# Second attention: weighing with the values standing in quarters of the array, and the order of VectorE's first counts and maxima

## The chip, the cores and the metric

One core of a Trainium2 chip runs the whole program. The metric is the device time of one execution in microseconds. Each kernel is run several times, and the median is taken. One more execution is recorded by the hardware profiler.

## The reference

Four transformer layers run one after the other on x of 8 batches, 256 tokens and 128 features, each an attention and a feed-forward stage behind an adaptive layer norm. The change lies in the attention of the second layer, here "the second attention":

```python
scores = einsum('bhqd,bhkd->bhqk', q, k) / sqrt(8)       # 16 heads of 8 features
attn = softmax(scores)
keep = rank_of(attn) < k_keep[head]                      # the k_keep largest of each row of 256
w = where(keep, attn, 0)
w = w / (sum(w) + 1e-10)
out = einsum('bhqk,bhkd->bhqd', w, v) @ Wo.T + bo
```

`k_keep` is a number per head, worked out from two small inputs. The other seven stages are untouched, but for two semaphores of the second layer pair's feed-forward stage that get another name.

## The kernel before

Every stage has its work written out by hand for each engine, in a fixed order, and the engines meet through semaphores. TensorE is PE in the rows, VectorE DVE, ScalarE ACT and GpSimd POOL.

**The second attention** is a pipeline over the batches. The loop `for n in range(-1, B)` stands in `l1_attn` of each engine. In the pass of n the engines work on four batches at once: n is weighed, n+1 has its thresholds searched, n+2 gets its scores, maxima and exponentials, and n+3 is projected. A batch has 16 heads and 2 tiles of 128 queries, so 32 blocks ("rows" in the code) of 128 queries by 256 keys.

- **The search** finds for each row of attention a threshold with k_keep values above it, up to a window of 8. It counts three times: VectorE counts six blocks (`count_below`, L3085), ScalarE the other 26 (`l1_count`, L4235). Behind the first count VectorE works out the next threshold in `first_move` (L3093), behind the second and third in `narrow` (L3105). Each of them waits until ScalarE has ended its counts. Then VectorE takes the final count with flags (`count_kept`, L3156), and `doubt` (L3168 to L3172) counts the rows whose count missed the window.
- **The doubts.** TensorE sums these over the partitions (`l1_doubt`, L1765). VectorE copies the sum to an integer (`ask_doubt`, L3177, then a memset L3179), loads it into a register and branches (`settle_doubt`): over a long bisection that is not needed with these inputs, to a line that raises two semaphores. Behind it `settle_doubt` writes `past` (L3192) and raises `over_ready`, which TensorE's `l1_turn` (L1671) waits for.
- **The marks.** Of each group of 4 blocks `largest_of` takes the eight largest candidates (MAX8, L3200), `all_but_past` (L3206) leaves those that are too many, and `mark` (L3212) marks them. `mark(n, 0)` needs `past`.
- **Turning and weighing.** `l1_turn_probs` (L1744, L1745) turns the probabilities of a head and takes away what is marked, and ScalarE's `l1_take_probs` (L4246) brings them to SBUF as `probsT`, in two buffers that take turns. `l1_weigh` (L1758) multiplies: for each of 2 query tiles and 2 key tiles the 128x128 piece of `probsT` is loaded as the standing operand, and 9 columns (8 of the values and a one, which gives the sum) move through. An f32 product is two instructions, so a head is eight. The result lies in bank 1 with the queries in the partitions.
- **The end of a batch.** VectorE's `weighed` (L3222 to L3226) divides by the sum, `l1_turn_out` and `l1_project_out` (L1778) project, and `l1_result` (L3233) hands over to GpSimd.
- **The order of a pass.** On VectorE the pass of n began with `largest_of(n, 0)`, `largest_of(n, 1)`, `ask_doubt(n)`, `settle_doubt(n)`, `all_but_past`, `mark(n, 0)`, then `l1_max(n+2, 0)` (L3072), `count_below(n+1, 0)`, `first_move(n+1)` and `weighed(n-1)`. On TensorE it begins with `l1_doubt(n)`, directly behind `l1_weigh(n-1, 15)`. On ScalarE it begins with the last of batch n+1's first counts, from block 20 on.

The waits of `l1_take_probs(b, h)`: for the turned head, and for `l1_weigh(b, h-2)`, which frees the buffer. ScalarE's exponentials of head h (`l1_exps`, L4185) wait for `l1_max` of that head on VectorE.

Of the kernel before, what the change touches and what calls it, by code (L numbers as in the profile page):

```python
# [11 lines left out]
ALU = mybir.AluOpType  # L12
# [3 lines left out]
P = 128  # L16
B, S, D = 8, 256, 128
T = S // P
H = 16
# [39 lines left out]
GROUP_WORDS = 4 * S // 2  # L59

# [124 lines left out]
def adaln_program(nc, x_in, c_in, const_in, ali_in, weights_in, out):  # L185
    ctx = ExitStack()
    with ctx:
# [287 lines left out]
        minus_two = silu_b[:, 0:P // 2].bitcast(BF16)  # L475
        first_rows = front_n[:].rearrange("p t d -> p (t d)")
# [131 lines left out]
        z_psum = signal("z_psum", l2_ffn=1)  # L608
        z_ready = signal("z_ready", l2_ffn=1)
# [645 lines left out]
        def _(pe):  # L1255
# [492 lines left out]
            def l1_weigh(b, h, ph="l1_attn"):  # L1748
# [5 lines left out]
                wide = HD + 1  # L1754
                for t in range(T):
                    for k in range(T):
                        at = t * S + k * P
                        last = mm(pb[1][:, t * S + h * wide:t * S + (h + 1) * wide], probsT[:, h % 2, at:at + P],  # L1758
                                  values_of(b, k)[:, h * wide:(h + 1) * wide], start=k == 0, stop=k == T - 1)
                last.then_inc(pv_done.sem, 1)  # L1760
# [20 lines left out]
            def l1_attn(ph="l1_attn"):  # L1781
# [10 lines left out]
                for n in range(-1, B):  # L1792
                    if now(n):
                        l1_doubt(n)
                    if now(n + 2):
                        l1_values(n + 2)
# [36 lines left out]
                    if now(n):  # L1833
                        l1_weigh(n, 4)
# [40 lines left out]
                    if now(n):  # L1875
                        l1_turn_probs(n, 13)
                        l1_weigh(n, 11)
                        l1_weigh(n, 12)
                        l1_turn_probs(n, 14)
# [3 lines left out]
                        l1_weigh(n, 15)  # L1883
                l1_turn_out(B - 1)
# [171 lines left out]
            def l2_fall(p, ph="l2_ffn"):  # L2056
# [3 lines left out]
                last.then_inc(z_psum.sem, 1)  # L2060

            def l2_out(p, ph="l2_ffn"):

                pe.wait_ge(pass_done.sem, pass_done(ph, p, 1))
                pe.wait_ge(z_ready.sem, z_ready(ph, p, 1))
# [240 lines left out]
        def _(dve):  # L2306
# [908 lines left out]
            def weighed(b, ph="l1_attn"):  # L3215
                dve.wait_ge(pv_done.sem, pv_done(ph, b, H))
                if b:
                    dve.wait_ge(turned.sem, turned(ph, b - 1, 1))
                wide = H * (HD + 1)
                o1 = tiles(pb[1])[:, :, 0:wide].rearrange("p t (h d) -> p t h d", h=H)  # L3220
                sums_by_tile = sums_of(b).rearrange("p h t -> p t h")
                link(V_.scalar_tensor_tensor(kept_sum, sums_by_tile, 1e-10, o1[:, :, :, HD], ALU.mult, ALU.add))  # L3222
# [3 lines left out]
                V_.tensor_tensor(tokens1.rearrange("p t (h d) -> p t h d", h=H), o1[:, :, :, 0:HD],  # L3226
# [1451 lines left out]
```

## Time and profile before

| | |
|---|---|
| median of 3 runs | 2046.71 us (2041.7 to 2064.53) |
| the profiled execution | 2043.58 us, of which span 2041.8 us |
| busy share of the span: PE, DVE, ACT, POOL | 80%, 72%, 55%, 43% |
| the second attention | about 493 to 1109 us of the span |
| one pass of it, in the middle | 70.4 to 71.0 us |

The busy shares are over stages with different limits. The second attention must be read from its own passes.

### The profile page before, as it was taken

How to read it: one execution, taken by the hardware profiler on the slowest of the kernel's cores; microseconds unless marked ns; L12 is line 12 of the kernel's file. 1: busy time of each engine (PE TensorE's matmuls, PEld its weight loads, DVE VectorE, ACT ScalarE, POOL GpSimd, SP SyncE). 2: the span in 40 equal slices, each digit the busy share in tenths (PEclk: the TensorE clock that was granted, in tenths of full speed). 3: DMA queues.
4: the chain of work that ended last, by engine and by line, in shares of the span. 5: the costliest groups of instructions: out<-in, count | busy, mean ns of one | idle time of the engine just before them, and what ended most of it. 6: DMA issues, size and time to landing. Idle time of an engine off the chain costs nothing.

```text
span 2041.8 us, 38862 instructions
## 1 busy us (share of the span) xinstructions
PE 1642.0 (80%) x12640; PEld 1172.7 (57%) x12640; DVE 1476.3 (72%) x4747; ACT 1115.7 (55%) x3322; POOL 877.4 (43%) x1162
## 2 busy tenths in 40 slices
PE   3888989897358988988779978527777799999978
PEld 3445667675236766766668645413443477777763
DVE  6678776555588988999887842358876777887657
ACT  2444444445988898899852423214452366666620
POOL 3333221124253554444433577676300377767610
PEclk8889999997555555555557989858896899999969
DMA  4111101003000000000001023322110000000000
GB/s 139 47 47 41 40 21 42 18 2 122 15 9 17 12 13 11 17 9 9 1 1 59 23 78 110 97 65 73 48 72 20 15 1 1 2 1 2 1 1 21
DMA packets 67305, 67.58 MB, mean 33 GB/s; under 512 B 9955, under 2 KB 58966, under 8 KB 66566
## 3 DMA queue, kind: packets, MB, share of 16 engines
q1 hardware_dynamic: 58930, 53.09, 7.9%
q0 software_dynamic: 5120, 10.50, 2.0%
q8 instruction: 104, 1.70, 0.4%
q10 hardware_dynamic: 3040, 1.38, 0.2%
q14 instruction: 111, 0.91, 0.2%
HBM read 30.41 MB, written 8.39 MB: 19 GB/s over the span
## 4 chain that ended last, share of the span: by engine, by line
PE 35%; DVE 27%; ACT 12%; issue 10%; POOL 6%; SPq 6%; ACTq 2%; DMA 1%; DVEq 0%; POOLq 0%
SPq L689 5%; POOL weights L1165 4%; DVE weights L3212 3%; PE bank L2143 3%; PE bank L1551 3%; PE bank L2103 3%; ACT big L4445 3%; PE bank L1567 3%; DVE weights L3156 3%; DVE nmax L3072 2%; DVE small L3200 2%; PE bank L1758 2%; PE bank L2130 2%; ACT rope_s L4235 2%; ACT rope_c L4235 2%
## 5 line engine op out<-in xcount | busy, mean ns | idle before, releaser
L1758 PEld LDWEIGHTS bank<-V,probsT 128*128 128x128 f32 x1024 | 203.6, 297 | 28.4 <-ACT probsT L4246 13.7
L1758 PE MATMUL bank<-V,probsT 128*128 128x9 f32 x1024 | 205.4, 333 | 15.2 <-ACT probsT L4246 10.9
L2711 DVE TENSOR_REDUCE nmax<-bank 128x4 f32<-128x1024 f32 x144 | 175.9, 1221 | 51.8 <-PE bank L1331 48.8
L891 POOL TENSOR_TENSOR big<-big,rinv 128x512 f32<-128x512 f32 x128 | 131.7, 1049 | 45.7 <-DVE rinv L3767 45.7
L1745 PE MATMUL bank<-silu_b,weights 128*128 128x128 bf16 x464 | 138.9, 303 | 0.0
L4050 ACT ACTIVATE feat_o<-bank 128x1024 f32<-128x1024 f32 x72 | 73.7, 1023 | 101.5 <-PE bank L1331 66.7
L4050 ACT ACTIVATE O<-bank 128x1024 f32<-128x1024 f32 x72 | 73.7, 1024 | 97.2 <-PE bank L1331 70.6
L3761 DVE TENSOR_REDUCE nmax<-bank 128x2 f32<-128x512 f32 x128 | 81.9, 682 | 58.1 <-PE bank L2103 58.1
L4445 ACT ACTIVATE big<-bank,nmax 128x256 f32<-128x256 f32 x256 | 117.6, 478 | 11.1 <-DVE nmax L3761 11.1
L4453 ACT ACTIVATE big<-bank 128x512 f32<-128x512 f32 x128 | 73.8, 614 | 68.8 <-PE bank L2130 68.8
L4246 ACT ACTIVATE probsT<-bank 128x512 f32<-128x512 f32 x128 | 75.9, 600 | 58.4 <-PE bank L1745 39.0
L1165 POOL DMA_INDIRECT weights<-h_rows,V x96 | 91.7, 955 | 32.2 <-issue 28.9
L1729 PE MATMUL bank<-qT 48*128 48x256 bf16 x256 | 62.8, 387 | 44.1 <-ACT weights L4185 34.2
L1744 PE MATMUL bank<-const,big 128*128 128x128 f32 x256 | 86.4, 417 | 8.7 <-DVE weights L3212 7.7
L3072 DVE TENSOR_REDUCE nmax<-bank 128x2 f32<-128x512 f32 x128 | 84.1, 681 | 9.3 <-PE bank L1729 9.3
L2143 PE MATMUL bank<-big,V 128*64 128x256 f32 x512 | 69.4, 390 | 16.9 <-ACT V L4460 15.7
L3537 DVE TENSOR_TENSOR O<-O,bank 128x512 f32<-128x512 f32 x24 | 16.5, 687 | 90.1 <-ACT O L4369 82.9
L4109 ACT ACTIVATE hid<-bank,weights 128x256 f32<-128x256 f32 x128 | 52.5, 470 | 48.5 <-PE bank L1551 48.4
L2130 PE MATMUL bank<-const,big 128*128 128x128 f32 x512 | 75.0, 279 | 2.5 <-POOL big L891 1.7
L1744 PEld LDWEIGHTS bank<-const,big 128*128 128x128 f32 x256 | 59.4, 232 | 29.6 <-DVE weights L3212 9.9
L1173 POOL DMA_INDIRECT weights<-y_rows,V x64 | 61.8, 966 | 29.8 <-issue 16.9
L2130 PEld LDWEIGHTS bank<-const,big 128*128 128x128 f32 x512 | 56.6, 141 | 29.0 <-issue 16.5
(818 smaller groups left out, 5110.5 us busy)
## 6 DMA issues: line engine op xcount, KB each, us to landing
qT<-parts SPq DMA_DIRECT2D x276, 32.0 KB
big<-V SPq DMA_DIRECT2D x192, 32.0 KB
y_rows<-weights SPq DMA_DIRECT2D x24, 256.0 KB, 2.3
big<-parts SPq DMA_DIRECT2D x180, 32.0 KB
weights<-in_weights_l_ffn SPq DMA_DIRECT2D x1, 4832.0 KB, 14.3
weights<-in_weights_l_attn SPq DMA_DIRECT2D x1, 3904.0 KB, 13.0
qT<-V SPq DMA_DIRECT2D x96, 32.0 KB
weights<-in_weights_l_ffn SPq DMA_DIRECT2D x1, 2860.0 KB, 11.7
```

Source lines behind the costliest of these rows:

```text
L689: queue.dma_start(stacks[m % STACKS][to, u * HALF:(u + 1) * HALF], pair_of(m, at, *of)).then_inc(stack_in[u].sem, 16)
L891: nc.gpsimd.tensor_tensor(row, row, rinv[:, h % H, :].unsqueeze(2).to_broadcast([P, T, S]), ALU.mult).then_inc(scaled.sem, 1)
L1165: nc.gpsimd.indirect_dma_start(gathered[i % RING1][:, t, :], None, h_rows, bass.IndirectOffsetOnAxis(ap=token_of[:, at:at + 1], axis=0)).t ...
L1744: mm(pb[6 + h % 2][:, at], row_of(b, 2 * h + t)[:, keys], C("ident"), start=True, stop=False, is_transpose=True)
L1745: last = mm(pb[6 + h % 2][:, at], unkept(b, g)[:, 2 * (h % 2) + t, keys], minus_two, start=False, stop=True)
L1758: last = mm(pb[1][:, t * S + h * wide:t * S + (h + 1) * wide], probsT[:, h % 2, at:at + P], values_of(b, k)[:, h * wide:(h + 1) * wide], s ...
L2130: last = nc.tensor.transpose(pb[TURN_BANKS3[h % 2]][:, k * S + t * P:k * S + (t + 1) * P], probs3[h % PROBS3][:, t * S + k * P:t * S + (k ...
L2143: last = mm(pb[7][HD3 * i:HD3 * (i + 1), w * S:(w + 1) * S], values3(q, k, 2 * w + i), probsT3[(4 * q + 2 * w + i) % TURNED3][:, k * S:(k ...
L2711: V_.tensor_reduce(to, scored.rearrange("p (i a n) -> p i a n", i=HPG, n=n), AX.X, ALU.max, negate=True).then_inc(score_max.sem, 1)
L3072: V_.tensor_reduce(nmax[:, h, :], tiles(pb[2 + n % 3]), AX.X, ALU.max, negate=True).then_inc(max_ready.sem, 1)
L4050: nc.scalar.activation(turned_probs[n % TURNS], turned_scores, ACT.Exp).then_inc(turned_exp.sem, 1)
L4445: last = nc.scalar.activation(probs3[h % PROBS3][:, t * S:(t + 1) * S], pb[h % 4][:, t * S:(t + 1) * S], ACT.Exp, bias=nmax[:, h % H, t:t ...
```

## The change

Three things, all in the second attention.

1. `l1_weigh` has the operands the other way round: the values of a head (128 keys x 9) stand, in the column quarter `h % 4` of the array, and the 256 queries of `probsT` move. Two products per head instead of four, four instructions instead of eight. The result has the features in the partitions: four heads share columns 0 to 255 of bank 1.
2. So every four heads ("a quad") ScalarE copies these 256 columns to SBUF (`l1_take_quad`), and TensorE turns them back with two products (`l1_turn_quad`), where the standing operand is 128x128 of the copy and 36 columns of the identity move. The first three quads go to columns 256 on of bank 1, the last to columns 0 on. The next quad's first `l1_weigh` stands behind `l1_turn_quad` on TensorE, and that waits for the copy. The last quad is copied and turned at the start of the next pass, behind `l1_doubt`. `weighed` reads two places, so it has five instructions instead of three.
3. On VectorE the pass begins with `count_below(n+1, 0)`, then `ask_doubt(n)`, then the eight maxima of `largest_of`, then `settle_doubt(n)`.

On TensorE `l1_turn_probs(n, 14)` moves ahead of `l1_weigh(n, 12)`.

```diff
+        weighed_quad = V[:, 0, 576:576 + S]
+        early_heads = 3 * H // 4
+        weighed_at = ((slice(0, early_heads), pb[1][:, S:S + T * early_heads * (HD + 1)]),
+                      (slice(early_heads, H), pb[1][:, 0:T * (H - early_heads) * (HD + 1)]))
...
-        z_psum = signal("z_psum", l2_ffn=1)
-        z_ready = signal("z_ready", l2_ffn=1)
+        side_psum = signal("side_psum", l1_attn=QUADS, l2_ffn=1)
+        side_taken = signal("side_taken", l1_attn=QUADS, l2_ffn=1)
...
             def l1_weigh(b, h, ph="l1_attn"):
...
-                for t in range(T):
-                    for k in range(T):
-                        at = t * S + k * P
-                        last = mm(pb[1][:, t * S + h * wide:t * S + (h + 1) * wide], probsT[:, h % 2, at:at + P],
-                                  values_of(b, k)[:, h * wide:(h + 1) * wide], start=k == 0, stop=k == T - 1)
+                wide, part = HD + 1, slice(32 * (h % 4), 32 * (h % 4) + HD + 1)
+                by_keys = probsT[:, h % 2, :].rearrange("p (t k n) -> p k t n", t=T, k=T)
+                for k in range(T):
+                    last = mm(pb[1][part, 0:S].rearrange("p (t n) -> p t n", t=T), values_of(b, k)[:, h * wide:(h + 1) * wide], by_keys[:, k],
+                              start=k == 0, stop=k == T - 1)
                 last.then_inc(pv_done.sem, 1)
+
+            def l1_turn_quad(b, q, ph="l1_attn"):
+                pe.wait_ge(side_taken.sem, side_taken(ph, b, q + 1))
+                of_heads = C("ident").rearrange("p (j d) -> p j d", j=4)[:, :, 0:HD + 1]
+                heads_there, there = weighed_at[q // 3]
+                at = 4 * q - heads_there.start
+                for t in range(T):
+                    o = there.rearrange("p (t h d) -> p t h d", t=T, d=HD + 1)[:, t, at:at + 4, :]
+                    last = mm(o, weighed_quad[:, t * P:(t + 1) * P], of_heads, start=True, stop=True)
+                last.then_inc(side_psum.sem, 1)
...
                     if now(n):
                         l1_doubt(n)
+                    if now(n - 1):
+                        l1_turn_quad(n - 1, QUADS - 1)
...
+                        l1_turn_quad(n, 0)
                         l1_weigh(n, 4)
...
                         l1_turn_probs(n, 10)
+                        l1_turn_quad(n, 1)
                         l1_weigh(n, 8)
...
                         l1_turn_probs(n, 13)
                         l1_weigh(n, 11)
+                        l1_turn_probs(n, 14)
+                        l1_turn_quad(n, 2)
                         l1_weigh(n, 12)
-                        l1_turn_probs(n, 14)
                         l1_turn_probs(n, 15)
                         l1_weigh(n, 13)
...
                 for n in range(-1, B):
+                    if now(n + 1):
+                        count_below(n + 1, 0)
                     if now(n):
+                        ask_doubt(n)
                         largest_of(n, 0)
                         largest_of(n, 1)
-                        ask_doubt(n)
                         settle_doubt(n)
                         all_but_past(n, 0)
                         mark(n, 0)
                     if now(n + 2):
                         l1_max(n + 2, 0)
                     if now(n + 1):
-                        count_below(n + 1, 0)
                         first_move(n + 1)
...
+            def l1_take_quad(b, q, ph="l1_attn"):
+                act.wait_ge(pv_done.sem, pv_done(ph, b, 4 * q + 4))
+                nc.scalar.activation(weighed_quad, pb[1][:, 0:S], ACT.Copy).then_inc(side_taken.sem, 1)
...
                         l1_count(n + 1, 0, 20, 21)
+                    if now(n - 1):
+                        l1_take_quad(n - 1, QUADS - 1)
...
+                        l1_take_quad(n, 0)
                         l1_take_probs(n, 5)
...
+                        l1_take_quad(n, 1)
                         l1_take_probs(n, 9)
...
                         l1_exps(n + 2, 14)
                     if now(n):
+                        l1_take_quad(n, 2)
                         l1_take_probs(n, 14)
```

## Rows read from the trace of the kernel before

**Rows 1.** The page, part 2: the granted TensorE clock in 40 equal slices.

```profile
PEclk8889999997555555555557989858896899999969
```

**Rows 2.** Window of one pass: busy PE, PEld, DVE, ACT, POOL, then granted clock.

```profile
862.40:932.80 70.40, 63.20 (x322) 50.66 (x322) 64.23 (x268) 63.30 (x243) 33.03 (x42) 0.54 0.04 13
```

**Rows 3.** Timeline of DVE at a pass's start: start, length, line, idle before.

```profile
862.32 0.19 DVE L3172 TENSOR_SCALAR_CACHE_REDUCE small<-small 128x32 f32<-128x32 f32 x1
862.43 2.71 DVE L3200 MAX8 small<-hid 128x8 f32<-128x256 f32 x8
866.10 0.14 DVE L3177 CAST doubts_i<-bank 1x1 int32<-1x1 f32 x1 [0.96 <-PE bank L1765]
...
870.01 0.42 DVE L3192 TENSOR_TENSOR weights<-const,small 128x256 f32<-128x256 f32 x1 [3.64 <-DVEq L3189]
...
872.91 0.47 DVE L3085 TENSOR_SCALAR_CACHE_REDUCE scale_b<-weights,front_n 128x256 bf16<-128x256 f32 x1
...
875.52 0.19 DVE L3093 TENSOR_TENSOR front_n<-front_n,routes 128x32 f32<-128x32 f32 x1
```

**Rows 4.** Timeline of DVE: the same instruction as the first, one pass later.

```profile
932.70 0.19 DVE L3172 TENSOR_SCALAR_CACHE_REDUCE small<-small 128x32 f32<-128x32 f32 x1
```

**Rows 5.** Timeline of PE at the same pass's start; heads 14 and 15 turned first.

```profile
857.15 0.45 PE L1744 MATMUL bank<-const,kT 128*128 128x128 f32 x1
...
859.91 1.82 PE L1758 MATMUL bank<-V,probsT 128*128 128x9 f32 x8
862.36 3.58 PE L1758 MATMUL bank<-V,probsT 128*128 128x9 f32 x16 [0.62 <-ACT probsT L4246]
865.87 0.19 PE L1765 MATMUL bank<-main_square,ones 128*1 128x1 f32 x2
...
870.58 0.66 PE L1671 MATMUL bank<-const,xb 128*128 128x128 f32 x2 [3.37 <-DVE weights L3192]
```

**Rows 6.** Timeline of ACT: exponentials of head 13, `l1_take_probs` 14, a 128x256 copy.

```profile
854.36 0.47 ACT L4185 ACTIVATE O<-bank,nmax 128x256 f32<-128x256 f32 x1 [2.13 <-DVE nmax L3072]
...
861.72 0.58 ACT L4246 ACTIVATE probsT<-bank 128x512 f32<-128x512 f32 x1
...
881.67 0.38 ACT L4215 ACTIVATE feat<-bank 128x256 f32<-128x256 f32 x1
```

**Rows 7.** Timelines of ACT and DVE: ends of second and third counts, `narrow` behind each.

```profile
891.15 0.21 ACT L4235 ACTIVATION_READ_ACCUMULATOR rope_s<-kT,small 128x1 f32 x1
...
892.62 0.19 DVE L3105 TENSOR_TENSOR small<-small,routes 128x32 f32<-128x32 f32 x1
...
910.08 0.54 ACT L4235 ACTIVATE rope_c<-kT,small 128x256 bf16<-128x256 f32 x1
...
911.92 0.18 DVE L3105 TENSOR_TENSOR small<-small,routes 128x32 f32<-128x32 f32 x1
```

**Rows 8.** Timeline of PE: f32 products of other shapes, in this stage and in others.

```profile
906.92 0.87 PE L1702 MATMUL bank<-probs,kT 128*128 128x16 f32 x4
907.64 1.85 PE L1758 MATMUL bank<-V,probsT 128*128 128x9 f32 x8
...
1855.65 1.03 PE L2091 MATMUL bank<-next_feat,weights 128*128 128x256 f32 x4
1856.52 1.03 PE L2114 MATMUL bank<-weights,feat 128*128 128x256 f32 x4
...
309.08 0.64 PE L1404 MATMUL bank<-O,big 128*32 128x256 f32 x8
309.65 2.05 PE L1519 MATMUL bank<-const 128*128 128x128 f32 x16
```

**Rows 9.** Timeline of PE in the last pass: the clock granted is full here.

```profile
1086.70 1.91 PE L1758 MATMUL bank<-V,probsT 128*128 128x9 f32 x16
```

**Rows 10.** Windows behind TensorE's restart at 870.58, with the granted clock.

```profile
870.00:876.00 6.00, 5.17 (x26) 3.51 (x27) 5.75 (x27) 4.78 (x19) 0.00 (x0) 0.50 0.00 1
876.00:877.00 1.00, 0.79 (x3) 0.29 (x2) 0.93 (x5) 1.00 (x4) 0.63 (x3) 0.89 0.00 0
```

More of the change, by code:

```diff
@@ L59 @@
 GROUP_WORDS = 4 * S // 2
+QUADS = H // 4
 QUICK_STEPS = 3
@@ L1753, in l1_weigh @@
                 pe.wait_ge(probsT_ready.sem, probsT_ready(ph, b, h + 1))
-                wide = HD + 1
-                for t in range(T):
-                    for k in range(T):
-                        at = t * S + k * P
-                        last = mm(pb[1][:, t * S + h * wide:t * S + (h + 1) * wide], probsT[:, h % 2, at:at + P],
-                                  values_of(b, k)[:, h * wide:(h + 1) * wide], start=k == 0, stop=k == T - 1)
-                last.then_inc(pv_done.sem, 1)
+                wide, part = HD + 1, slice(32 * (h % 4), 32 * (h % 4) + HD + 1)
[3 more added lines that the diff above has]
+                              start=k == 0, stop=k == T - 1)
+                last.then_inc(pv_done.sem, 1)
+            def l1_turn_quad(b, q, ph="l1_attn"):
[3 more added lines that the diff above has]
+                at = 4 * q - heads_there.start
+                for t in range(T):
+                    o = there.rearrange("p (t h d) -> p t h d", t=T, d=HD + 1)[:, t, at:at + 4, :]
+                    last = mm(o, weighed_quad[:, t * P:(t + 1) * P], of_heads, start=True, stop=True)
+                last.then_inc(side_psum.sem, 1)
             def l1_doubt(b, ph="l1_attn"):
@@ L1883, in l1_attn @@
                         l1_weigh(n, 15)
+                l1_turn_quad(B - 1, QUADS - 1)
                 l1_turn_out(B - 1)
@@ L2059, in l2_fall @@
                     last = mm(pb[6][:], W(ph, "win2")[:, c * P:(c + 1) * P], gelus(c), start=c == 0, stop=c == O2 - 1)
-                last.then_inc(z_psum.sem, 1)
+                last.then_inc(side_psum.sem, 1)
             def l2_out(p, ph="l2_ffn"):
                 pe.wait_ge(pass_done.sem, pass_done(ph, p, 1))
-                pe.wait_ge(z_ready.sem, z_ready(ph, p, 1))
+                pe.wait_ge(side_taken.sem, side_taken(ph, p, 1))
                 for j in range(2 * T):
@@ L3215, in weighed @@
             def weighed(b, ph="l1_attn"):
-                dve.wait_ge(pv_done.sem, pv_done(ph, b, H))
+                dve.wait_ge(side_psum.sem, side_psum(ph, b, QUADS))
                 if b:
                     dve.wait_ge(turned.sem, turned(ph, b - 1, 1))
-                wide = H * (HD + 1)
-                o1 = tiles(pb[1])[:, :, 0:wide].rearrange("p t (h d) -> p t h d", h=H)
                 sums_by_tile = sums_of(b).rearrange("p h t -> p t h")
-                link(V_.scalar_tensor_tensor(kept_sum, sums_by_tile, 1e-10, o1[:, :, :, HD], ALU.mult, ALU.add))
+                for of, there in weighed_at:
+                    o1 = there.rearrange("p (t h d) -> p t h d", t=T, d=HD + 1)
+                    link(V_.scalar_tensor_tensor(kept_sum[:, :, of], sums_by_tile[:, :, of], 1e-10, o1[:, :, :, HD], ALU.mult, ALU.add))
                 linkup()
@@ L3225, in weighed @@
                 linkup()
-                V_.tensor_tensor(tokens1.rearrange("p t (h d) -> p t h d", h=H), o1[:, :, :, 0:HD],
-                                 kept_sum.unsqueeze(3).to_broadcast([P, T, H, HD]), ALU.mult).then_inc(tok_ready.sem, 1)
+                for of, there in weighed_at:
+                    o1 = there.rearrange("p (t h d) -> p t h d", t=T, d=HD + 1)
+                    heads_there = of.stop - of.start
+                    last = V_.tensor_tensor(tokens1.rearrange("p t (h d) -> p t h d", h=H)[:, :, of], o1[:, :, :, 0:HD],
+                                            kept_sum[:, :, of].unsqueeze(3).to_broadcast([P, T, heads_there, HD]), ALU.mult)
+                    if of.stop == H:
+                        last.then_inc(tok_ready.sem, 1)
+                    else:
+                        link(last)
             def l1_result(b, ph="l1_attn"):
@@ L4347, in l1_attn @@
                         l1_count(n + 2, 0, 17, 20)
+                l1_take_quad(B - 1, QUADS - 1)
                 l1_take_out(B - 1)
@@ L4424, in l2_ffn @@
             def l2_ffn(p, ph="l2_ffn"):
-                act.wait_ge(z_psum.sem, z_psum(ph, p, 0))
+                act.wait_ge(side_psum.sem, side_psum(ph, p, 0))
                 for c in range(O2):
```

4 lines of the change are left out of this document (2 added, 2 removed).

## The prediction

> **What bounds the kernel now.** I read the clock by slices first, then one middle pass of the second attention in the windows, then VectorE's timeline at its start, then TensorE's and ScalarE's. The clock stands at its lower level, 1.2 GHz, almost throughout this stage [rows 1], so TensorE's prices here are doubled. In a pass of 70.4 us three engines are nearly full: TensorE 63.2 us, VectorE 64.2, ScalarE 63.3 [rows 2]. No busy share names the bound; the waits do. Call D the moment when VectorE has the doubts counted and starts the eight maxima (862.43), and P the moment when TensorE's sum of them is there (866.10). VectorE needs 2.7 us for the maxima, waits 0.96 us for P, and behind the copy stands idle 3.64 us for the load and the branch [rows 3]. These 4.6 us are nearly all its idle time in a pass. P is late because TensorE still weighs heads 14 and 15 until 865.9, and it had waited 0.62 us for ScalarE to bring head 14 [rows 5]. ScalarE had waited 2.13 us for VectorE's maximum of head 13, some 8 us before D [rows 6]. So the loop is VectorE, ScalarE, TensorE, VectorE.
>
> ScalarE has little room elsewhere. It ends its second counts at 891.36 and its third at 910.6, and VectorE comes for them at 892.62 and 911.92 [rows 7]: 1.3 us of slack each.
>
> **VectorE's order.** Before, from D to `first_move` it is 13.1 us (862.43 to 875.52) [rows 3]: maxima, wait, copy, branch, `past`, marks, `l1_max`, and last `count_below` with 2.6 us (872.91 to 875.52). After, `count_below` covers the wait instead of the maxima, and the maxima run while the sequencer loads and branches. From P to `first_move` it was 9.4 us; without the count 6.8, and 0.1 for issuing eight maxima: 6.9. The time from D is then (P-D) + 6.9, as long as P-D is over 2.6. With P-D at 3.67 as before this would be 10.6, a gain of 2.5 us a pass. It is lost once P-D reaches 6.2. That the sequencer goes on while maxima are queued isn't shown by a row of a branch; bounds are 0 and 2.7 us covered, and I take the full cover, as nothing behind the maxima waits for them before `past`.
>
> **What weighing costs.** A head is now 4 instructions with 256 moving columns. In the fourth layer four f32 instructions of that shape follow each other in 0.87 us at full clock (1855.65 to 1856.52) [rows 8], so 1.74 at half. Before, a head was half of 3.5 us at half clock [rows 5] and half of 1.9 minus the tail, 0.88, at full [rows 9]. So turning the operands round saves TensorE nothing: it was bound by loading 128 columns eight times, and is bound now by moving 256 four times. Changing between the whole array and a quarter: in the first attention eight such instructions in four quarters take 0.57 us (309.08 to 309.65) [rows 8] where two rounds of 0.22 are 0.43; so 0.1 each time, taken as 0.13 for a head. New is `l1_turn_quad`, four instructions with a 128-column load: the nearest row has four with 16 columns in 0.72 (906.92 to 907.64) [rows 8], I take 0.9 at half clock. Per pass +3.6 and +2.0, on 63.2: TensorE would be full in 69 us at the lower clock.
>
> ScalarE gets four copies of 0.38 us [rows 6]. VectorE gets two more small instructions in `weighed`, 0.2 us. The renamed semaphores cost nothing: the same waits. No DMA and no queue of SP or GpSimd is passed by a moved step.
>
> **The new handshake, where I see the price.** `l1_take_quad(n, 2)` stands behind ScalarE's exponentials of head 14, where `l1_take_probs` 14 started at 861.72 [rows 6]. ScalarE can't come sooner: it waits for VectorE's maximum of head 13, and works from there without a pause. The copy ends at 862.1, D minus 0.3. Only then may TensorE turn the quad, and behind this in its queue stand weigh 12, turn 15, and weigh 13, 14 and 15, and then the doubts' sum. Before, only 14 and 15 were left at this time. At half clock: 0.9 + 1.87 + 1.38 (two heads were turned in 2.76, 857.15 to 859.91 [rows 5]) + 1.87 + 3.6 = 9.6 us, so P-D = -0.3 + 9.6 + 0.2 = 9.4. At full clock half of it, P-D = 4.7. ScalarE waits too: `l1_take_probs` 14 needs weigh 12, and `l1_take_quad` 3 needs weigh 15.
>
> The clock: 256 columns now move where 9 did, and stages with such weighing have it full [rows 1], so I expect it to be full in more of the pass. But TensorE, having turned head 14, stands idle for the copy, several us at full clock. Behind the like pause at 870.58 it ran at the lower level until about 876 [rows 5, 10], 5.5 us. I take that: 5.5 us of the 9.6 at half, the other 4.1 in 2.05. P-D = 7.4. Then `first_move` is at D + 14.3, 1.2 later than before.
>
> **What is late next.** ScalarE goes on only from P, and needs 44.5 us from P to the end of its third counts (866.10 to 910.6) [rows 3, 7]; plus 0.5 for copies and the later start. VectorE would be at its `narrow` sooner behind P than before and waits. From there it has 20.9 us to the next D [rows 4, 7]. So a pass is P-D + 44.5 + 0.5 + 0.1 + 20.9 = P-D + 66.0: 73.4 us, 3.0 more than 70.4.
>
> **The sum**, against the profiled execution (2043.58 us, 3.1 under the median of 2046.71). Five passes, n = 1 to 5, have everything: +15.0. In n = 6 ScalarE has no exponentials and only the 1.2 + 0.2 count: +1.4. Pass 0 has no weighing ahead of its doubts, so the cover works, but ScalarE's slack of 1.3 less one copy lets through 0.9: -0.9. The doubts of pass 7: -2.0 of the 2.7. Behind them TensorE alone sets the end. There 14 or so heads at full clock cost 0.13 more, three quads 0.5 each, and copy, turn and two waits 1.2 at the end; against it the clock rises some us sooner: -1.8 (from -2.3 to +20, were it to stay low). In all +11.7: **2055 us**.
>
> Against this stands a rule of the Trainium skill (TensorEngine Tiling (Array Packing), Key Properties): tiles in different columns load and multiply in parallel. By it heads 13, 14 and 15, in three quarters and next to each other, would overlap. It is a rival below. The same list says that changing the tiling mode drains the engine; the row puts that at 0.1 us, so it changes little.
>
> **Rivals.**
> - *The clock stays low* (slower; 0.22). A product in one quarter may not lift it. P-D = 9.4, a pass 75.4: five times 5.0, pass 6 +6.2 as TensorE is full there, -0.9, -2.0: +28, 2072 us. It decides from P-D = 6.2 up. For it: this stage alone never had the clock. Against: the other weighing stages have it.
> - *The branch isn't covered* (slower; 0.08). `first_move` at P + 9.6, a pass 74.5, and passes 0 and 7 lose their gain: +23, 2067 us.
> - *Full clock at once* (0.12). P-D = 4.7, a pass 70.7: five times 0.3, pass 6 -1.3, -0.9, -4.3: 2039 us.
> - *The quarters overlap* (0.07). Eight instructions in 0.57 us [rows 8] instead of 1.74 show what neighbours can do. Three heads in the time of one, 3.6 us less at half clock: P-D = 5.6, a pass 71.6: +0.5, 2044 us. Against: each head's four stay in one quarter.
> - *The handshake isn't late* (faster; 0.13). Were ScalarE at its copy 4 us earlier, P-D would be 2.6 or less. ScalarE's counts are then the bound: 0.7 to 1.9 us less a pass: five times 1.9, pass 6 -3.6, -0.9, -4.3: -18, 2025 us.
>
> **How the numbers follow.** The forecast has 0.38. A change within 1% (20 us) can't be told from none here. Faster by more needs the last rival and something beside it, 0.14 with what I may have missed. Slower by more, over 2067: most of the low clock, half of the uncovered branch, some of the forecast's upper part: 0.27. The rest, 0.59, is within. The range goes from the fast rival to the low clock with part of the last pass: 2026 to 2080.
>
> **What would show it.** After: L1765 some 7 us behind D instead of 3.7, with VectorE's wait for it 4 us or more; a wait of ScalarE at L4246 for L1758 of about 3 us in front of head 14; idle time between the maxima and L3192 of about 1.3 us instead of 3.64; small waits at L3105; the clock above 0.55 in the pass. Wrong would be the forecast if ScalarE's copy of quad 2 comes well ahead of D, if TensorE has the full clock when it arrives, or if VectorE's maxima end long before L3192.

## Result and profile after

The changed kernel takes 2066.73 us, the median of 20 runs (2060.29 to 2071.63), beside 2050.95 us (2041.06 to 2064.53, 20 runs) for the kernel before: a ratio of 1.008, 95% interval 1.0063 to 1.0096. The profiled execution took 2064.9 us, its span 2063.1. The forecast was 2055 us, within 1%.

The page's clock by slices ([rows 1] has those of before), and from its costliest groups the weighing, the turn of a quarter (new) and `l1_take_probs` with the idle time ahead of them. (A "quarter" of the heads is the quad of the code, which counts from 0: quad 2 is the third quarter, heads 8 to 11.)

```profile
PEclk9899999997567777777688989857887899999969
...
L1762 PE MATMUL bank<-probsT,V 128*9 128x256 f32 x512 | 157.4, 469 | 23.3 <-ACT probsT L4274 23.0
...
L4274 ACT ACTIVATE probsT<-bank 128x512 f32<-128x512 f32 x128 | 76.2, 601 | 74.0 <-PE bank L1762 53.9
...
L1773 PE MATMUL bank<-const,V 128*128 128x36 f32 x128 | 29.3, 368 | 82.5 <-ACT V L4278 82.5
```

TensorE's mean granted clock over the stage is 0.73 now instead of 0.57, and it stands 82.5 us in all for ScalarE's copies of the quarters. The windows of the whole stage (busy PE, PEld, DVE, ACT, POOL, then clock), before:

```profile
480.00:1135.00 655.00, 521.19 (x2758) 415.43 (x2757) 557.96 (x2288) 521.66 (x1959) 276.70 (x354) 0.57 0.07 23
```

and after:

```profile
480.00:1135.00 655.00, 434.68 (x2268) 231.64 (x2266) 541.69 (x2259) 520.69 (x1969) 270.90 (x350) 0.73 0.06 21
```

TensorE is 87 us less busy, and the kernel is slower. VectorE's timeline of pass 4, the counterpart of [rows 3]: the doubts' count, the copy of their sum, the maxima, `past`, `first_move`, the narrowings, and the maxima of later scores.

```profile
868.88 0.18 DVE L3192 TENSOR_SCALAR_CACHE_REDUCE small<-small 128x32 f32<-128x32 f32 x1
...
876.28 0.15 DVE L3197 CAST doubts_i<-bank 1x1 int32<-1x1 f32 x1 [4.80 <-PE bank L1779]
...
876.59 2.71 DVE L3220 MAX8 small<-hid 128x8 f32<-128x256 f32 x8
880.46 0.43 DVE L3212 TENSOR_TENSOR weights<-const,small 128x256 f32<-128x256 f32 x1 [1.16 <-DVEq L3209]
...
884.99 0.19 DVE L3113 TENSOR_TENSOR front_n<-front_n,routes 128x32 f32<-128x32 f32 x1 [1.54 <-ACTq L4267]
...
902.50 0.19 DVE L3125 TENSOR_TENSOR small<-small,routes 128x32 f32<-128x32 f32 x1 [0.55 <-ACTq L4267]
...
922.11 0.19 DVE L3125 TENSOR_TENSOR small<-small,routes 128x32 f32<-128x32 f32 x1 [0.24 <-ACTq L4267]
...
926.04 1.29 DVE L3092 TENSOR_REDUCE nmax<-bank 128x2 f32<-128x512 f32 x2 [1.01 <-PE bank L1734]
```

These six waits are 9.30 us. The pass takes 75.13 us (868.88 to 944.01), so 65.83 without them. Before, it took 70.38 with 4.60 of waits [rows 3, 4], 65.78 without. **A pass is VectorE's 65.8 us and its waits**, in both kernels. The branch's cover works (1.16 instead of 3.64), but the wait for the sum grew from 0.96 to 4.80, and four waits came up that weren't there.

TensorE at the same place, to be held against [rows 5]: turn of quad 2, weigh 12, weigh 13 and 14 together, the first product of weigh 15, turn of quad 3.

```profile
868.73 1.07 PE L1773 MATMUL bank<-const,V 128*128 128x36 f32 x4 [7.58 <-ACT V L4278]
869.73 1.88 PE L1762 MATMUL bank<-probsT,V 128*9 128x256 f32 x4
...
873.01 1.43 PE L1762 MATMUL bank<-probsT,V 128*9 128x256 f32 x8
875.17 0.39 PE L1762 MATMUL bank<-probsT,V 128*9 128x256 f32 x1 [0.74 <-ACT probsT L4274]
...
878.79 0.64 PE L1773 MATMUL bank<-const,V 128*128 128x36 f32 x4 [2.59 <-ACT V L4278]
```

And ScalarE, against [rows 6]: copy of quad 2, `l1_take_probs` 14 and 15, copy of quad 3, its last count.

```profile
868.30 0.37 ACT L4278 ACTIVATE V<-bank 128x256 f32<-128x256 f32 x1
871.70 0.60 ACT L4274 ACTIVATE probsT<-bank 128x512 f32<-128x512 f32 x1 [3.03 <-PE bank L1762]
...
874.52 0.60 ACT L4274 ACTIVATE probsT<-bank 128x512 f32<-128x512 f32 x1 [1.74 <-PE bank L1762]
...
878.37 0.37 ACT L4278 ACTIVATE V<-bank 128x256 f32<-128x256 f32 x1
...
884.32 0.50 ACT L4263 ACTIVATE rope_c<-kT,front_n 128x256 bf16<-128x256 f32 x1
```

TensorE stands 7.58 us for a copy that ends at 868.67, 0.2 before the doubts' count. ScalarE then stands 3.03 and 1.74 us for TensorE, and only behind that come its counts, the last at 884.8, just ahead of `first_move`. Two windows of TensorE behind its restart, in the columns as above; the clock was at 0.50 from 864 on:

```profile
870.00:872.00 2.00, 2.00 (x7) 0.69 (x6) 1.48 (x8) 0.30 (x1) 0.00 (x0) 0.50 0.00 0
...
874.00:876.00 2.00, 1.26 (x10) 0.38 (x6) 0.00 (x0) 1.48 (x6) 0.00 (x0) 1.00 0.00 0
```

### The profile page after: what moved, and what is told of

Its sections match the earlier page's. It is cut to its first block, busy times and chain, and to the rows that moved or that the text cites. A ratio compares the mean times of both kernels' runs of the same rounds, so it can differ in the third digit from the quotient of the medians.

```text
span 2063.1 us, 38143 instructions
## 1 busy us (share of the span) xinstructions
PE 1575.1 (76%) x12256; PEld 1003.5 (49%) x12256; DVE 1481.8 (72%) x4763; ACT 1125.2 (55%) x3354; POOL 877.6 (43%) x1162
## 4 chain that ended last, share of the span: by engine, by line
PE 36%; ACT 23%; DVE 17%; issue 9%; POOL 6%; SPq 5%; ACTq 2%; DMA 1%; DVEq 0%; POOLq 0%
ACT rope_s L4263 5%; ACT rope_c L4263 5%; SPq L694 5%; POOL weights L1170 4%; PE bank L2163 3%; PE bank L2123 3%; ACT big L4483 3%; PE bank L1556 3%; PE bank L1572 3%; DVE weights L3176 3%; PE bank L1762 2%; PE bank L2150 2%; DVE nmax L2731 2%; PE bank L2111 2%; ACT big L4213 2%
## 5 line engine op out<-in xcount | busy, mean ns | idle before, releaser
L1762 PE MATMUL bank<-probsT,V 128*9 128x256 f32 x512 | 157.4, 469 | 23.3 <-ACT probsT L4274 23.0
L1750 PE MATMUL bank<-silu_b,weights 128*128 128x128 bf16 x464 | 110.7, 259 | 0.0
L1773 PE MATMUL bank<-const,V 128*128 128x36 f32 x128 | 29.3, 368 | 82.5 <-ACT V L4278 82.5
L1734 PE MATMUL bank<-qT 48*128 48x256 bf16 x256 | 52.1, 340 | 45.2 <-ACT weights L4213 32.6
L1762 PEld LDWEIGHTS bank<-probsT,V 128*9 128x9 f32 x512 | 38.3, 101 | 93.9 <-issue 40.2
L3565 DVE TENSOR_TENSOR O<-O,bank 128x512 f32<-128x512 f32 x24 | 16.5, 688 | 90.2 <-ACT O L4407 78.3
L2150 PE MATMUL bank<-const,big 128*128 128x128 f32 x512 | 75.1, 279 | 2.5 <-POOL big L896 1.7
L1749 PE MATMUL bank<-const,big 128*128 128x128 f32 x256 | 69.7, 353 | 7.4 <-DVE weights L3232 3.8
L1360 PE MATMUL bank<-big 57*128 57x128 bf16 (+1 forms) x512 | 42.7, 271 | 38.2 <-DVE nmax L2731 24.2
```

Of the source, the lines that this page charges most:

```text
L1750: last = mm(pb[6 + h % 2][:, at], unkept(b, g)[:, 2 * (h % 2) + t, keys], minus_two, start=False, stop=True)
L1762: last = mm(pb[1][part, 0:S].rearrange("p (t n) -> p t n", t=T), values_of(b, k)[:, h * wide:(h + 1) * wide], by_keys[:, k], start=k == 0, ...
L2150: last = nc.tensor.transpose(pb[TURN_BANKS3[h % 2]][:, k * S + t * P:k * S + (t + 1) * P], probs3[h % PROBS3][:, t * S + k * P:t * S + (k ...
```

## Experiments

In the table D is the start of the doubts' count, P that of the copy of their sum (VectorE's timelines), the stage the time from the first D to the eighth; distances are of pass 4. Ratios are to the kernel before, measured beside each.

| kernel | median us | ratio, interval | stage | P-D | `first_move`-D |
|---|---|---|---|---|---|
| before | 2050.95 | | 484.5 | 3.78 | 13.2 |
| changed | 2066.73 | 1.008, 1.0063 to 1.0096 | 511.0 | 7.40 | 16.1 |
| e1 VectorE's order alone | 2050.32 | 0.9986, 0.9955 to 1.0016 | 482.7 | 2.51 | 10.6 |
| e2 weighing alone | 2074.15 | 1.0117, 1.0076 to 1.0157 | 510.9 | 7.50 | 17.0 |
| e3 third copy early | 2030.84 | 0.9913, 0.9884 to 0.9942 | 477.4 | 2.97 | 10.9 |
| e4 wait filled | 2048.92 | 0.9985, 0.9956 to 1.0014 | 493.0 | 5.08 | 13.8 |
| e5 counts, exponentials ahead | 2074.55 | 1.011, 1.0068 to 1.0152 | 515.4 | 8.89 | 16.2 |
| e6 sum ahead | 2069.76 | 1.0097, 1.0062 to 1.0132 | 510.0 | 2.51 | 16.5 |
| e7 e5 and e6 | 2067.11 | 1.0084, 1.0053 to 1.0115 | 506.1 | 2.51 | 16.0 |
| e8 e3, old order | 2038.58 | 0.994, 0.9914 to 0.9966 | 480.7 | 2.74 | 12.1 |
| e9 counts ahead | 2063.52 | 1.0074, 1.0047 to 1.01 | 507.4 | 7.42 | 14.5 |
| e10 e9 and e6 | 2055.86 | 1.0033, 1.0009 to 1.0058 | 497.8 | 2.52 | 14.4 |
| e12 before, last pass filled | 2048.35 | 1.0011, 0.9986 to 1.0036 | 484.0 | 3.78 | 13.2 |
| e13 e3, second copy early | 2035.56 | 0.9926, 0.9898 to 0.9954 | 475.2 | 2.52 | 10.8 |

**The two parts apart.** To the kernel before only VectorE's new order was given:

```diff
+                    if now(n + 1):
+                        count_below(n + 1, 0)
                     if now(n):
+                        ask_doubt(n)
                         largest_of(n, 0)
                         largest_of(n, 1)
-                        ask_doubt(n)
                         settle_doubt(n)
...
-                        count_below(n + 1, 0)
                         first_move(n + 1)
```

> The kernel before with VectorE's new order alone: the first count and the doubts' count, then the two maxima, then the doubts' copy and the branch; TensorE's and ScalarE's programs are those of before. Theory A (the order gives its cover, but the pass is then held by ScalarE's counts and by TensorE's scores): the idle time of the branch falls from 3.64 to about 1.2 us a pass, first_move starts 1 to 2.5 us sooner after the doubts' count, and the whole comes out 5 to 12 us under the kernel before, 2039 to 2046. Rival B (the branch was hidden by nothing and everything behind it moves up): 2.5 us a pass more than that is not to be had, but all of 3.64 - 1.16 = 2.5 us in each of 7 passes is, 17 us, 2034. Rival C (the handoff of the doubts is late in any order): no change, 2051.

`first_move` comes 2.6 us sooner in pass 4, but the stage is only 1.8 us shorter and the whole can't be told from before. The median is rival C's, but not for its reason: in passes 1, 3, 5 and 6 P-D is 3.8 to 4.3, much as before (2.9 to 4.3), and yet `first_move` comes 1.3 to 3.8 us sooner in each pass but pass 3, whose branch is long (below). A's gain is there and is mostly waited away: in pass 4 waits for ScalarE of 0.91 and 0.59 and one of 0.69 for TensorE take its place. Passes 1, 2 and 4 are 1.2 to 1.8 us shorter than before, pass 3 is 2.0 longer. Then the changed kernel with the old order (the same diff backwards):

> The changed kernel with VectorE's old order (maxima first, then the doubts' count, the branch, then the first count), so the weighing change alone. Theory A (the quarter's turn on TensorE holds up the doubts' sum, and the new order wins back about 1 to 2.5 us a pass of it): the wait for the doubts' sum is 4 to 6 us as the doubts' count comes later, first_move comes 1 to 2.5 us a pass later than in the changed kernel, the whole is 5 to 12 us over it, 2072 to 2079. Rival B (once TensorE is the late one, VectorE's order is worth nothing): within 2 us of the changed kernel, 2067.

```profile
882.57 0.15 DVE L3197 CAST doubts_i<-bank 1x1 int32<-1x1 f32 x1 [4.68 <-PE bank L1779]
...
886.51 0.43 DVE L3212 TENSOR_TENSOR weights<-const,small 128x256 f32<-128x256 f32 x1 [3.66 <-DVEq L3209]
...
932.33 1.29 DVE L3092 TENSOR_REDUCE nmax<-bank 128x2 f32<-128x512 f32 x2 [1.01 <-PE bank L1734]
```

These are all its waits in pass 4, 9.35 us beside the changed kernel's 9.30. The stage is 510.9 us beside 511.0: in it the new order is worth nothing, which is B's mechanism. It turned 2.5 us of branch into 2.3 us of waiting for ScalarE. But the median is 7.4 us over the changed kernel's, which is A's range and not B's. The profiled spans differ by 8.8 us: 6.1 lie before the first D, 1.5 in the last pass (from D to `weighed` 41.9 us instead of 40.4), 1.3 behind it. The 6.1 need not be the order's, for two profiles with the same code up to there, of the kernel before and of e12, have their first D at 578.1 and at 571.8. So the order's worth in the whole stays open: nothing in passes 0 to 6 of these profiles, 1.5 us in the last.

**The late copy.** One call moved on ScalarE:

```diff
                         l1_exps(n + 2, 13)
+                    if now(n):
+                        l1_take_quad(n, 2)
+                    if now(n + 2):
                         l1_start(n + 2)
...
                     if now(n):
-                        l1_take_quad(n, 2)
                         l1_take_probs(n, 14)
```

> The changed kernel with one call moved on ScalarE: the copy of the third quarter (heads 8 to 11) stands right behind the exponentials of head 13, ahead of the counts 5 to 14, instead of behind those of head 14. Theory A (the loss is the 7.5 us in which TensorE stands before the turn of the quarter, the probabilities of head 15 and the doubts' sum behind it): that idle time is gone, the doubts' sum comes about 3 us after VectorE's count instead of 7.4 to 8.2, the pass falls from 75.4 to about 70 us and the whole is 25 to 35 us under the changed kernel, 2032 to 2042. Rival B (the low clock under quarters is what is late, the wait only takes its place): the wait is gone but the turns and weighings of heads 12 to 15 still run at half clock for 6 to 7 us, a gain of 5 to 10 us, 2057 to 2062. Rival C (the counts on ScalarE set the pass): the copy's wait moves to ScalarE and the counts end no sooner, within 3 us of the changed kernel.

VectorE's first three waits in pass 4 (0.78, 0.24 and 1.01 follow, 4.28 in all beside 9.30):

```profile
852.53 0.15 DVE L3197 CAST doubts_i<-bank 1x1 int32<-1x1 f32 x1 [0.38 <-remote]
...
856.72 0.42 DVE L3212 TENSOR_TENSOR weights<-const,small 128x256 f32<-128x256 f32 x1 [1.16 <-DVEq L3209]
...
860.41 0.19 DVE L3113 TENSOR_TENSOR front_n<-front_n,routes 128x32 f32<-128x32 f32 x1 [0.71 <-ACTq L4267]
```

A holds, at 1 us under its range: the whole is 36 us below the changed kernel and, by its own comparison, 0.6 to 1.2% below the kernel before. So the copy's place carries all of the loss. e8 is e3 with VectorE's old order:

> The kernel with the third quarter's copy moved forward, with VectorE's old order (maxima, doubts' count, branch, then the first count): the weighing by quarters without the late copy and without VectorE's new order. Theory A (with the copy in time, VectorE is late, and its new order is worth what it covers of the branch less what it then waits for ScalarE): idle before the pass's second tile of work is 3.7 us instead of 1.2, no wait for ScalarE at first_move and at the narrowings (0.71, 0.78, 0.24 before), so 0.6 to 1.2 us a pass more, the whole 3 to 9 us over the 2031 of the kernel with the early copy, 2034 to 2040. Rival B (the new order is worth all of the 2.5 us that it covers): 17 us over it, 2048.

7.7 us over e3 by the medians, 3.3 in the stage: A by its total. With the copy in time, VectorE's order is worth something, though not the 2.5 us a pass that it covers, and not A's 0.6 to 1.2 us in each pass: 2.9 of the 3.3 lie in pass 1, where the branch is long (below).

**Clock or order?** On TensorE, between the turn of head 14 and that of the quarter, products whose result nobody reads:

```diff
                         l1_turn_probs(n, 14)
+                        if now(n + 2):
+                            for _ in range(28):
+                                mm(pb[0][:, 0:P], C("ident"), C("ident"), start=True, stop=True)
                         l1_turn_quad(n, 2)
```

> The changed kernel with 28 products of the identity by itself (128 x 128, into a bank of the scores, read by nobody) on TensorE between the turn of head 14 and the turn of the quarter, in each pass where they fit: they fill some 2 to 3 us of the 7.5 us in which TensorE stands there, so that the clock has less idle time before the heads 12 to 15. Theory A (the clock's part of the handoff is small beside the order's): the copy by ScalarE comes no sooner, the handoff gets 0 to 2 us shorter where the clock is at 1.00, the whole comes out 0 to 12 us under the changed kernel, 2055 to 2067. Rival B (the clock is the main part): the handoff falls from 7.5 to about 5 us, 17 us and more under it, 2050 or less.

TensorE in pass 4: the useless products, the turn of quad 2, weigh 12, weigh 13 and 14.

```profile
857.03 6.47 PE L1899 MATMUL bank<-const 128*128 128x128 f32 x56
864.79 0.64 PE L1773 MATMUL bank<-const,V 128*128 128x36 f32 x4 [1.28 <-ACT V L4281]
865.35 1.03 PE L1762 MATMUL bank<-probsT,V 128*9 128x256 f32 x4
...
867.15 1.04 PE L1762 MATMUL bank<-probsT,V 128*9 128x256 f32 x8
```

My theory A misses: it is B that holds. The products fill 6.47 of the 7.58 us, not the 2 to 3 that I expected, and the granted clock stays at 1.00 from 857.0 to 870.0 in this profile. The copy comes no sooner, yet P-D falls by 2.32 us, since the same work runs at 2.4 GHz (1.03 for weigh 12 instead of 1.88). Of the 3.62 us by which P-D had grown, 2.3 are the price of restarting at 1.2 GHz behind the idle time. The pass is 3.2 us shorter, since the maxima's later wait of 1.01 goes too. With 28 useless products in a pass the kernel is 18 us faster than the changed one.

**Is the sum of the doubts the late one?** On TensorE the sum goes ahead of the turn of the quarter:

```diff
-                    if now(n):
+                    if n == 0:
                         l1_doubt(n)
...
                         l1_turn_probs(n, 14)
+                        if now(n + 1):
+                            l1_doubt(n + 1)
                         l1_turn_quad(n, 2)
```

> The changed kernel with TensorE's sum of the doubts ahead of the turn of the third quarter, so that it no longer stands behind the work of heads 12 to 15. ScalarE and VectorE as in the changed kernel. Theory A (two chains are late behind the copy, the doubts' sum and ScalarE's counts, and ScalarE's ends as late): the sum comes 2.5 us behind VectorE's count instead of 7.5, but first_move waits some 6.5 us for ScalarE instead of 1.54, still 16 us behind the doubts' count; the pass stays within 0.5 us of 75.2, the whole within 4 us of the changed kernel, 2063 to 2071. Rival B (the handoff of the doubts is what costs the time, as the forecast's sum had it): the pass falls with it by 4 to 5 us to about 70.5, the whole to 2035 to 2045.

VectorE's two longest waits in pass 4, for scores and for the counts:

```profile
881.83 0.69 DVE L3094 TENSOR_REDUCE nmax<-bank 128x2 f32<-128x512 f32 x1 [2.92 <-PE bank L1734]
...
886.29 0.19 DVE L3115 TENSOR_TENSOR front_n<-front_n,routes 128x32 f32<-128x32 f32 x1 [3.77 <-ACTq L4269]
```

P-D is down by 4.9 us and nothing is gained: VectorE waits 6.7 us for scores and counts instead, and `first_move` stands where it did. A, in its numbers. So the sum's path is one of two that are late together.

**ScalarE's counts.** First its five counts and the exponentials of head 15 went ahead of its copies of heads 14 and 15:

```diff
                         l1_take_quad(n, 2)
-                        l1_take_probs(n, 14)
                     if now(n + 2):
-                        l1_count(n + 2, 0, 15, 16)
+                        l1_count(n + 2, 0, 15, 17)
+                        l1_exps(n + 2, 15)
+                        l1_count(n + 2, 0, 17, 20)
                     if now(n):
+                        l1_take_probs(n, 14)
                         l1_take_probs(n, 15)
-                    if now(n + 2):
-                        l1_count(n + 2, 0, 16, 17)
-                        l1_exps(n + 2, 15)
-                        l1_count(n + 2, 0, 17, 20)
```

> The changed kernel with ScalarE's order at the pass's end changed: behind the copy of the third quarter it does the counts 15 to 19 and the exponentials of head 15 first (3.4 us of work), and the copies of the probabilities of heads 14 and 15 behind them, in the time in which it stood 3.0 and 1.7 us for TensorE. TensorE and VectorE as in the changed kernel. Theory A (first_move waits 1.54 us for counts that ScalarE does only after it stood for TensorE's turns; this is the term that the forecast left out): first_move's wait is gone, the copy of head 15 and the doubts' sum come up to 0.3 us later, the pass gets 1.2 us shorter, the whole 5 to 10 us, 2057 to 2062. Rival B (what follows the handoff is VectorE's own work, the wait named for ScalarE is a by-product): first_move at the same distance from the doubts' sum, within 3 us of the changed kernel, 2067.

> Both edits: ScalarE's counts ahead of its copies of heads 14 and 15, and TensorE's sum of the doubts ahead of the turn of the third quarter. Theory A (ScalarE's chain is the one that is left: copy of the quarter, heads 14 and 15, the last quarter's copy, the norms and 11 counts): first_move comes 14 us behind the doubts' count instead of 16.1, with 4 us of wait for ScalarE; the pass is 2 us shorter, the whole 9 to 15 us under the changed kernel, 2052 to 2058. Rival B (the sum alone): as low as 2035 to 2045. Rival C (no chain but the clock matters): within 3 us of the changed kernel.

ScalarE in e5, the exponentials of head 15:

```profile
879.61 0.47 ACT L4213 ACTIVATE kT<-bank,nmax 128x256 f32<-128x256 f32 x1 [3.52 <-PE bank L1750]
```

Both expectations missed, because of the edit (e7's median falls within 3 us of the changed kernel, as its rival C has it, but e7 says nothing on C's reason, the clock): the exponentials overwrite the buffer out of which TensorE still has to turn head 15, and that turn stands behind the quarter's. Their wait of 3.52 us (e5) held up both copies. e9 has the counts 15 to 19 ahead and the exponentials behind both copies; e10 has the early sum besides:

> The changed kernel with ScalarE's counts 15 to 19 ahead of its copies of the probabilities of heads 14 and 15, and the exponentials of head 15 behind the copy of head 15. In the run in which the exponentials stood ahead too they waited 3.52 us for TensorE's turn of head 15, whose buffer they overwrite, and held up both copies; here nothing that waits stands ahead of them. Theory A (first_move waits for counts that ScalarE could have done while it stood for TensorE): the doubts' sum stays 7.4 to 7.9 us behind VectorE's count, the counts end 6.6 us behind the sum instead of 8.5, first_move's wait of 1.54 is gone, the pass is 1.2 to 1.5 us shorter, the whole 6 to 10 us under the changed kernel, 2056 to 2061. Rival B (the wait is a by-product and comes back at the next thing): within 3 us of the changed kernel, 2067.

> The same order on ScalarE, and TensorE's sum of the doubts ahead of the turn of the third quarter. Theory A (the two late chains are the doubts' sum and ScalarE's counts; with the sum early ScalarE's chain alone is left, and it ends 14.3 us behind the doubts' count): first_move at 14.0 to 14.6 us instead of 16.5, the pass 2 us under the changed kernel's, the whole 11 to 16 us under it, 2051 to 2056, and 4 to 6 us under the kernel with the counts alone. Rival B (the sum's place is worth nothing at any time): as with the counts alone.

In e9 `first_move` has no wait, but the next narrowing has 1.58 instead of 0.55 us, and ScalarE stands for TensorE behind its counts:

```profile
904.04 0.19 DVE L3125 TENSOR_TENSOR small<-small,routes 128x32 f32<-128x32 f32 x1 [1.58 <-ACTq L4267]
```

```profile
886.62 0.60 ACT L4274 ACTIVATE probsT<-bank 128x512 f32<-128x512 f32 x1 [1.56 <-PE bank L1750]
```

The first narrowing stays 25.7 us behind P (26.2 in the changed kernel, 26.5 before): from P the branch, the marks, TensorE's turn and ScalarE's counts follow one another. So B's mechanism holds: the wait comes back at the next thing. The whole is 3.2 us under the changed kernel, just outside B's 3 and short of A's 6, with intervals that overlap. e10, with both, is 10.9 us under it, inside A's range, and its interval lies apart. So each of the two paths hides the other, and only both edits together bring a gain clear of the noise.

**One more copy.** e13 is e3 with the second quarter's copy moved as well:

```diff
                         l1_take_probs(n, 8)
+                        l1_take_quad(n, 1)
                     if now(n + 1):
                         l1_count(n + 1, 2, 25, ROWS1)
                     if now(n):
-                        l1_take_quad(n, 1)
                         l1_take_probs(n, 9)
```

> The kernel with the third quarter's copy moved forward, and the second quarter's too: on ScalarE it stands right behind the copy of head 8, ahead of the counts 25 to 32, instead of behind them. Theory A (the same as at the third quarter, in small: the late copy holds TensorE 2.98 us with the next scores behind it, and VectorE's maxima wait 1.01 us for them in pass 4 and not in passes 1 to 3): TensorE's wait there is under 1 us, the maxima's wait is gone where it was, and the pass is that much shorter, the whole 0 to 3 us under the kernel with one early copy, 2028 to 2031. Rival B (each wait taken from TensorE there is a wait in VectorE's passes): 1 us in each of 6 passes, 2025 or less. Rival C (the counts that now come later hold up the narrowing): 2 to 5 us over it, 2033 to 2036.

The maxima's wait in pass 4 is gone and the stage is 2.2 us shorter, as A has it. The whole isn't: 2035.56, in rival C's range, with an interval that overlaps e3's. C's reason isn't seen in the stage: the narrowings wait 1.06 us in pass 4 beside 1.02 in e3. e3 stays the version to take.

**The kernel before's spread.** The last pass in windows of 10 us, before (1082.54 on) and in e1 (1085.09 on), and where VectorE waits for the last weighing in e1:

```profile
1082.54:1092.54 10.00, 10.00 (x105) 9.68 (x104) 9.11 (x38) 3.58 (x6) 5.72 (x6) 1.00 0.01 2
1092.54:1102.54 10.00, 10.00 (x83) 9.43 (x81) 8.31 (x50) 3.23 (x6) 2.97 (x2) 0.78 0.00 0
```

```profile
1085.09:1095.09 10.00, 10.00 (x55) 9.25 (x55) 8.31 (x52) 1.79 (x3) 2.97 (x2) 0.50 0.01 2
1095.09:1105.09 10.00, 10.00 (x54) 9.25 (x55) 2.01 (x8) 2.15 (x4) 0.00 (x0) 0.50 0.00 0
```

```profile
1114.05 0.19 DVE L3222 SCALAR_TENSOR_TENSOR O<-colmax,bank 128x32 f32<-128x32 f32 x1 [16.95 <-PE bank L1758]
```

From the last D to there it is 43.1 us before and 59.0 in e1, with the same program on TensorE, busy all the time in both from 10 us behind D on: there only the clock differs. Such a pass takes e1's profile to 2055.2 although its stage is shorter. To see whether this makes the spread of the kernel before, its last pass was filled:

```diff
                         l1_doubt(n)
+                    if n == B - 1:
+                        for _ in range(28):
+                            mm(pb[3][:, 0:P], C("ident"), C("ident"), start=True, stop=True)
```

> The kernel before with 28 products of the identity by itself (128 x 128, into a bank of the scores, read by nobody) on TensorE behind the sum of the doubts of the last pass alone, where it stands 8.3 us (6.7 in another run) for VectorE's first marks. It looks at why the kernel before spreads over 28 us and the changed one over 11: in the profile of the kernel before the clock comes to 1.00 in the last pass 20 us behind the doubts' count, in that of the kernel with VectorE's order alone it stays at 0.50 to the end of the stage and the last weighing ends 15.9 us later by the same reading. Theory A (the last pass of the old weighing comes to either clock): with the idle time filled the clock is at 1.00 in the last pass in every run, the median falls by 5 to 12 us to 2037 to 2045 and the spread to 15 us or less. Rival B (the spread is from elsewhere): median and spread as before, 2047 to 2052 over 25 us.

In its profile the clock is 0.83 in the first 10 us of that pass and 0.98 to 1.00 in the next 30, and the last weighing ends 38.7 us behind D instead of 43.1. But the median is as before, and the runs go from 2040.12 to 2056.96. A fails for the median; the upper end came down from 2063.34, no more than a hint. The spread goes with the clock of the whole run all the same: of the 87 runs of the kernel before that stand beside the experiments, those under 2042.1 us have a mean granted clock of 0.791 to 0.800, those over 2060 us 0.779 to 0.786. That is an association and no experiment; in which stages the clock differs, apart from what the profiles show of the last pass, stays open.

## Why the prediction was right, and where its sum was off

**The handshake was read rightly.** The late copy, TensorE's idle time in front of it, the restart at the lower clock, ScalarE's 3 us in front of head 14, the branch's idle time and the small waits are all there. P-D is 7.40 in pass 4, or 7.29 from the forecast's own D, which is 0.11 us later, against 7.4. Since e3 takes it all back by moving one call, this cause is shown. That P-D came out to the tenth is luck in part: two things that the sum didn't have, the overlap of heads 13 and 14 and the wait for head 15 (last paragraph), nearly cancel. And the change is only just within 1%: the forecast drew that line at 2067, the median is 2066.73.

**The step that was mis-sized is "what is late next"**: ScalarE "goes on only from P". A pass was to be P-D + 66.0 and is P-D + 67.7 (75.13 - 7.40). By its parts:
- P to `first_move`: 6.9 forecast, 8.7 measured. ScalarE goes on not from P but from its copy of head 15, 1.8 us earlier, and with 3.4 us of counts and exponentials ahead of the last quarter's copy, which the forecast had finished by then. P to the second narrowing: 45.1 forecast, 45.8 measured. e2, e6, e9 and e10 show this path beside the sum's.
- From there to the next D: 20.9 forecast, 21.9 measured (75.13 - 7.40 - 45.83), of which 1.01 is the new wait for scores. It comes from the same mechanism at the second quarter, whose copy holds TensorE 2.98 us in pass 4; the forecast looked at the third quarter alone. e13 takes it away.
- In pass 0 the forecast was -0.9 and it was +0.3, in pass 6 +1.4 and +3.9, the whole growth of P-D there; passes 1 to 5 +22.3 instead of +15.0; the last pass, D to `weighed`, 40.4 instead of 43.1: -2.8 instead of -3.8.

Together the stage and the last pass are 23.8 us longer instead of 11.7. The profiled spans differ by 21.3, as the stage began 5.7 us sooner in the profile after and untouched code behind it took 3.3 us more. The medians differ by 15.8: the kernel before's profile, on which the sum stood, was 7.4 us under its median, that of after 1.8.

**The cover of the branch** was given full worth, and as an event it nearly has it: 2.5 of the 2.7 us. Its worth in time is nothing in passes 0 to 6 while ScalarE is late, by the profile of e2.

**The rivals.** The clock did not stay low: 0.73 in the stage. It was not at 1.00 at once either: it came up at 873.8, 5.1 us behind the restart at 868.73, where the forecast had 5.5. The handshake in time, priced at 2025, is e3 at 2031. The overlap of the quarters happens where two heads follow each other with nothing between: in e4 four products take 1.03 us and the eight of heads 13 and 14 take 1.04. The rule of the Trainium skill (TensorEngine Tiling (Array Packing), Key Properties), that different tiles work in parallel, agrees with that row; the forecast gave it 0.07 and its sum had no overlap. It took about one head off P-D, some 0.9 us as an estimate from the 1.03 of one alone, but head 15 came 0.74 us late from ScalarE and ran alone.

## What to carry to other kernels

When a step is split by a handshake through another engine, look at where the handshake stands in that engine's queue, and put it at the first place where its input is there: here the place of one line is worth 36 us. Of the engine that bounds a loop write down every wait of one pass; if the rest is the same in all variants (65.6 to 65.9 us in pass 4 of the 14 profiles here), the difference is in those waits, and removing one shows which stands behind it. Idle time of TensorE can cost a second time where its clock falls in it: here 2.3 us behind 7.6 us of it.

## What was not expected of the hardware

- The clock stayed at 0.50 for the whole of e1's last pass, with TensorE busy 10.00 of 10.00 us in 40 us of it, and came to 1.00 in the same code in the profile before, where it was back at 0.50 from 1098.5 on, 7.1 us ahead of the last weighing's end, with TensorE busy all the time as well. Being busy alone neither brought it up nor held it there; what decides isn't shown.
- Two heads in neighbouring quarters, eight f32 products of 256 columns, took 1.04 us where one head's four took 1.03.
- The branch takes longer in pass 1 of all 14 profiles: from the sum's copy to `past` 6.30 us in the kernel before, beside 3.91 in pass 4. With VectorE's old order that costs 2.2 to 2.4 us more than in pass 4; under the maxima 0.6 to 0.9 (idle 2.00 us in pass 1 and 1.16 in pass 4 of the changed kernel). In pass 3 of e1 it is 6.74 us under the maxima too, with 3.73 idle. The cause wasn't looked for.
